# Expert slots handed out in two phases, in a fused attention and mixture-of-experts kernel

## What is computed

```
x = x + conv_ref(ln_c(x))          # keys = queries, softmax over 256 positions, value, output
t = tokens(x);  n = ln_t(t)        # 2048 x 64
probs = softmax(n @ router_w.T);  the top 2 of 8, renormalised, are the gates
h = silu(n @ w1[e].T) * (n @ w3[e].T)      # 682 hidden units per expert
y = h @ w2[e].T
out = t + sum over the two chosen experts of gate * y
```

## Time and profile before

| | us |
|---|---|
| median of 3 runs | 226.94 (225.74 to 230.49) |
| the profiled execution | 226.59 |
| its span in the profile | 224.9 |
| PE busy | 154.0 (69%) |
| DVE busy | 112.0 (50%) |
| POOL busy | 85.5 (38%) |
| ACT busy | 72.3 (32%) |
| DMA moved | 33.47 MB, of it 39 weight loads of 576 KB |

### The profile page before, as it was taken

The page is one execution under the profiler, slowest core; times in us unless marked ns, Lnnn a source line. Parts: engine busy times, 40 slices in busy tenths (PEclk is TensorE's granted clock), DMA queues, the critical chain, the costliest instruction groups (busy, mean ns, idle before and its releaser), DMA issues.

```text
span 224.9 us, 4952 instructions
## 1 busy us (share of the span) xinstructions
PE 154.0 (69%) x1714; PEld 134.1 (60%) x1714; DVE 112.0 (50%) x398; ACT 72.3 (32%) x154; POOL 85.5 (38%) x109
## 2 busy tenths in 40 slices
PE   2647698795835000009999999999999999974040
PEld 2436598694734000007888888888888888862020
DVE  2696687679458640003544555454554545440050
ACT  2226544433001000005444445355444445530010
POOL 6142520204787777710003344333333444352300
PEclk9999755569555555555999999999999999997555
DMA  4999800000000000011067887887878887000153
GB/s 130 431 388 421 342 0 3 0 0 0 26 26 28 30 24 25 29 39 34 3 224 227 265 286 250 292 282 245 270 241 253 265 262 266 24 15 12 38 170 89
DMA packets 16315, 33.47 MB, mean 149 GB/s; under 512 B 7827, under 2 KB 9011, under 8 KB 15779
## 3 DMA queue, kind: packets, MB, share of 16 engines
q1 hardware_dynamic: 14018, 30.80, 40.6%
q0 software_dynamic: 2272, 2.36, 3.2%
HBM read 25.94 MB, written 7.21 MB: 147 GB/s over the span
## 4 chain that ended last, share of the span: by engine, by line
issue 40%; POOL 31%; DVE 11%; PE 9%; DMA 4%; ACT 3%; POOLq 1%; ACTq 0%; SPq 0%
POOL ys L335 16%; POOL xs L294 13%; PE bank L804 2%; DVE xn L478 2%; DMA y_in<-ys 2%; DVE kq_right L510 1%; DVE neg_max L515 1%; PE bank L754 1%; PE bank L770 1%; POOL rstd L278 1%; DMA x_sb<-x_tok 1%; ACT kq_right L355 1%; DMA ys<-y_out,y_row 1%; PE bank L792 1%; DVE t_sb L535 1%
## 5 line engine op out<-in xcount | busy, mean ns | idle before, releaser
L335 POOL DMA_INDIRECT ys<-y_out,y_row x39 | 37.5, 962 | 76.2 <-DVE y_out L722 70.2
L918 PE MATMUL bank<-x_cols,weights 64*128 64x128 f32 x468 | 64.5, 286 | 0.5 <-issue 0.5
L920 PE MATMUL bank<-x_cols,weights 64*128 64x128 f32 x468 | 64.5, 286 | 0.0
L714 DVE TENSOR_TENSOR hid<-bank,act_sb 128x512 f32<-128x512 f32 (+1 forms) x60 | 40.7, 678 | 45.8 <-ACT act_sb L429 36.9
L918 PEld LDWEIGHTS bank<-x_cols,weights 64*128 64x128 f32 x468 | 56.9, 193 | 7.4 <-issue 7.0
L920 PEld LDWEIGHTS bank<-x_cols,weights 64*128 64x128 f32 x468 | 56.9, 193 | 0.0
L429 ACT ACTIVATE act_sb<-bank 128x512 f32<-128x512 f32 (+1 forms) x60 | 35.3, 589 | 43.1 <-PE bank L918 42.3
L294 POOL DMA_INDIRECT xs<-rows,pos x32 | 31.2, 975 | 9.7 <-issue 9.7
L936 PE MATMUL bank<-hid,weights 128*64 128x128 f32 x468 | 30.8, 277 | 3.5 <-ACT y_cols L437 3.5
L936 PEld LDWEIGHTS bank<-hid,weights 128*64 128x64 f32 x468 | 25.8, 137 | 6.1 <-issue 3.8
L898 PE MATMUL bank<-ident,x_pairs 128*128 128x128 f32 x39 | 9.2, 317 | 26.7 <-issue 26.7
(11 more groups left out here) (123 smaller groups left out, 192.5 us busy)
## 6 DMA issues: line engine op xcount, KB each, us to landing
weights<-experts SPq DMA_DIRECT2D x39, 576.0 KB
xs<-zeros SPq DMA_DIRECT2D x4, 1056.0 KB, 8.8
x_in<-xs SPq DMA_DIRECT2D x39, 33.0 KB, 1.7
y_in<-ys SPq DMA_DIRECT2D x4, 256.0 KB, 4.0
ys<-y_out,y_row POOLq DMA_INDIRECT x39
xs<-rows,pos POOLq DMA_INDIRECT x32
out<-result SPq DMA_DIRECT2D x8, 64.0 KB, 2.1
x_sb<-x_tok SPq DMA_DIRECT2D x1, 384.0 KB, 3.6
```

Source lines behind the costliest of these rows:

```text
L335: nc.gpsimd.indirect_dma_start(ys, bass.IndirectOffsetOnAxis(ap=y_row[:, HALVES * i + h:HALVES * i + h + 1], axis=0), y_out[:, i % RING, h ...
L714: nc.vector.tensor_tensor(live(i, hid[:, g % HRING, :]), live(i, H3_BANK[g % 3][:]), live(i, act_sb[:, g % 3, :]), ALU.mult).then_inc(hid_ ...
L918: first_ = nc.tensor.matmul(H1_BANK[g % 2][:, dst], weights[0:C, slot, at:at + P], x_cols[0:C, i % 2, src], start=True, stop=True)
L920: second_ = nc.tensor.matmul(H3_BANK[g % 3][:, dst], weights[C:P, slot, at:at + P], x_cols[C:P, i % 2, src], start=True, stop=True)
```

## The change

The slots are handed out in two phases. Phase 0 opens slots 0 to 7 from the counts of blocks 0 and 1, the first half of the tokens. It gives them to subtiles that are full by then: at least 9 of the kind exist whatever the routing. Phase 1 opens slots 8 to 38 from the final counts, less what phase 0 has used. Both phases have a table, so all 39 slots now have their expert and row from value loads.

On SP, the weight loads of the first eight slots no longer go out at the start. After the first table is ready, SP does for each of pairs 0 to 3 four value loads, the weight loads, for pair 0 a wait for the scatters of blocks 0 and 1 (dispatched[0]), and the x_in loads. Then it waits for the second table, and pairs 4 to 19 follow in the order of before, the first of them with a wait for dispatched[1].

On DVE, the first table (subtiles_of_experts(0), owners_of_slots(0), rows_of_slots(0), 12 instructions) stands between positions(2) and choose(3). The second (used_up and what follows, 26 instructions) is cut in four parts, which stand in the expert stage behind multiply(0) and pair_up(2), multiply(1), multiply(3) and pair_up(3), and multiply(5). The rows of phase 0 are all filled, so that pairs 0 to 3 need no keep. On PE, rank(2) has one more small matmul for the counts, and rank_read and counts_ready are waited for before up(0). ACT preloads the table of silu. The number of slots, the work per slot, the scatters and their order on POOL, and the end are as before.

The diff, cut to its core:

```
--- before.py
+++ after.py
-NX = (K_TOP * CAP - 1) // SUB
-NS = E + NX
+NS = E + (K_TOP * CAP - 1) // SUB
 NT = -(-NS // HALVES)
-MORE = CAP // SUB - 1
+MOST = CAP // SUB
+
+
+KNOWN = (2, NBLK)
+PHASES = len(KNOWN)
+OPENED = (0, 8, NS)
+assert all(OPENED[p + 1] <= -(-(K_TOP * BLK * KNOWN[p] - E * (SUB - 1)) // SUB) for p in range(PHASES - 1))
...
+        def phase_of(k):
+            return next(p for p in range(PHASES) if k < KNOWN[p])
+
+        def pairs_of(p):
+            return range(-(-OPENED[p] // HALVES), -(-OPENED[p + 1] // HALVES))
...
-            for e in range(E):
-                sp.dma_start(weights[:, e, :], experts[e]).then_inc(w_loaded[e], 16)
-
-            sp.wait_ge(dispatched, 16 * TILES * K_TOP)
-            for j in range(E):
-                sp.dma_start(x_in[:, j // HALVES, j % HALVES, :], xs[CAP * j:CAP * j + SUB, :]
-                             ).then_inc(x_in_loaded[j // HALVES], 16)
-            sp.wait_ge(table_ready, 1)
-            for i in range(E // HALVES, NT):
-                owners = [sp.value_load(table[0:1, 0, HALVES * i + h - E:HALVES * i + h - E + 1],
-                                        min_val=0, max_val=E - 1) for h in halves(i)]
-                at = [sp.value_load(table[0:1, 1, HALVES * i + h - E:HALVES * i + h - E + 1],
-                                    min_val=0, max_val=E * CAP - SUB) for h in halves(i)]
-                if i >= XRING:
-                    sp.wait_ge(gated, i - XRING + 1)
-                for h in halves(i):
-                    sp.dma_start(x_in[:, i % XRING, h, :], xs[bass.ds(at[h], SUB), :]).then_inc(x_in_loaded[i % XRING], 16)
-                sp.wait_ge(hid_used, STEPS * (i - WSLOTS // HALVES + 1))
+
+            def load_weights(i, owners):
+                if i >= WSLOTS // HALVES:
+                    sp.wait_ge(hid_used, STEPS * (i - WSLOTS // HALVES + 1))
                 for h in halves(i):
                     s = (HALVES * i + h) % WSLOTS
                     sp.dma_start(weights[:, s, :], experts[bass.ds(owners[h], 1)].rearrange("o p c -> p (o c)")
                                  ).then_inc(w_loaded[s], 16)
+
+            for p in range(PHASES):
+                blocks = KNOWN[p] - (KNOWN[p - 1] if p else 0)
+                sp.wait_ge(table_ready, p + 1)
+                for i in pairs_of(p):
+                    owners = [sp.value_load(table[0:1, 0, HALVES * i + h:HALVES * i + h + 1],
+                                            min_val=0, max_val=E - 1) for h in halves(i)]
+                    at = [sp.value_load(table[0:1, 1, HALVES * i + h:HALVES * i + h + 1],
+                                        min_val=0, max_val=E * CAP - SUB) for h in halves(i)]
+                    if p == 0:
+                        load_weights(i, owners)
+                    if i == pairs_of(p)[0]:
+                        sp.wait_ge(dispatched[p], 16 * TPB * K_TOP * blocks)
+                    if i >= XRING:
+                        sp.wait_ge(gated, i - XRING + 1)
+                    for h in halves(i):
+                        sp.dma_start(x_in[:, i % XRING, h, :], xs[bass.ds(at[h], SUB), :]).then_inc(x_in_loaded[i % XRING], 16)
+                    if p > 0:
+                        load_weights(i, owners)
...
-                            rows[:, TPB * k + t, c, :], None).then_inc(dispatched, 16)
+                            rows[:, TPB * k + t, c, :], None).then_inc(dispatched[phase_of(k)], 16)
...
+            nc.scalar.preload_act_table(ACT.Silu)
...
+                for p in range(PHASES - 1):
+                    if KNOWN[p] == k:
+                        count(p, K_BANK[:, TPB * E:(TPB + 1) * E])
...
+            def count(p, sums):
+                nc.vector.tensor_tensor(taken_by[:, p, :], sums, base[:], ALU.subtract).then_inc(counts_ready, 1)
+
+            def subtiles_of_experts(p):
+                dve.wait_ge(counts_ready, p + 1)
+                last = p == PHASES - 1
+                dims = [P, E, MOST]
+                chain(nc.vector.scalar_tensor_tensor(out=over[:], in0=taken_by[:, p, :].unsqueeze(2).to_broadcast(dims),
+                                                     scalar=float(SUB - 1) if last else 0.0,
+                                                     in1=steps_sub[:].unsqueeze(1).to_broadcast(dims),
+                                                     op0=ALU.add, op1=ALU.is_ge))
+                chain(nc.vector.tensor_reduce(full[:], over[:], AX.X, ALU.add))
+                if p > 0:
+                    chain(nc.vector.tensor_tensor(full[:], full[:], used[:, p - 1, :], ALU.subtract))
+                chain(nc.vector.tensor_tensor(upto_full[:], upto[:], full[:].unsqueeze(1).to_broadcast([P, E, E]),
+                                              ALU.mult))
+                chain(nc.vector.tensor_reduce(ends[:], upto_full[:], AX.X, ALU.add))
+
+            def owners_of_slots(p):
+                own = slice(OPENED[p], OPENED[p + 1])
+                n = OPENED[p + 1] - OPENED[p]
+                chain(nc.vector.tensor_scalar(given[:], ends[:], float(SUB), None, ALU.mult))
+                end = given[:, 0:E - 1].unsqueeze(1).to_broadcast([P, n, E - 1])
+                chain(nc.vector.tensor_tensor(passed[:, own, :], slot_at[:, own].unsqueeze(2).to_broadcast([P, n, E - 1]),
+                                              end, ALU.is_ge))
+                chain(nc.vector.tensor_reduce(owner[:, own], passed[:, own, :], AX.X, ALU.add))
+                nc.vector.tensor_copy(table[:, 0, own], owner[:, own]).then_inc(dve_step, 1)
+                steps[0] += 1
+                chain(nc.vector.tensor_tensor(starts[:, own, :], passed[:, own, :], end, ALU.mult))
+                chain(nc.vector.tensor_reduce(first[:, own], starts[:, own, :], AX.X, ALU.max))
+                chain(nc.vector.tensor_tensor(row_at[:, own], slot_at[:, own], first[:, own], ALU.subtract))
+
+            def rows_of_slots(p):
+                own = slice(OPENED[p], OPENED[p + 1])
+                n = OPENED[p + 1] - OPENED[p]
+                all_e = [P, n, E]
+                if p == 0:
+                    nc.vector.scalar_tensor_tensor(out=table[:, 1, own], in0=owner[:, own], scalar=float(CAP),
+                                                   in1=row_at[:, own], op0=ALU.mult, op1=ALU.add).then_inc(table_ready, 1)
+                    return
+                chain(nc.vector.scalar_tensor_tensor(out=begin[:], in0=used[:, p - 1, :], scalar=float(SUB), in1=base[:],
+                                                     op0=ALU.mult, op1=ALU.add))
+                chain(nc.vector.tensor_tensor(of_owner[:, own, :], order[:].unsqueeze(1).to_broadcast(all_e),
+                                              owner[:, own].unsqueeze(2).to_broadcast(all_e), ALU.is_equal))
+                chain(nc.vector.tensor_tensor(starts_e[:, own, :], of_owner[:, own, :],
+                                              begin[:].unsqueeze(1).to_broadcast(all_e), ALU.mult))
+                chain(nc.vector.tensor_reduce(owned[:, own], starts_e[:, own, :], AX.X, ALU.add))
+                chain(nc.vector.tensor_tensor(owned[:, own], owned[:, own], row_at[:, own], ALU.add))
+                nc.vector.tensor_scalar(table[:, 1, own], owned[:, own], float(E * CAP - SUB), None, ALU.min
+                                        ).then_inc(table_ready, 1)
+
+            def used_up(p):
+                chain(nc.vector.tensor_scalar(given[:], ends[:], float(OPENED[p + 1] - OPENED[p]), None, ALU.min))
+                before_ = slice(0, E - 1)
+                if p == 0:
+                    chain(nc.vector.tensor_copy(used[:, p, :], given[:]))
+                else:
+                    chain(nc.vector.tensor_tensor(used[:, p, :], used[:, p - 1, :], given[:], ALU.add))
+                chain(nc.vector.tensor_tensor(used[:, p, 1:], used[:, p, 1:], given[:, before_], ALU.subtract))
+
+            def occupancy(p):
+                own = slice(OPENED[p], OPENED[p + 1])
+                n = OPENED[p + 1] - OPENED[p]
+                all_e = [P, n, E]
+                chain(nc.vector.scalar_tensor_tensor(out=left[:], in0=used[:, p - 1, :], scalar=-float(SUB),
+                                                     in1=taken_by[:, p, :], op0=ALU.mult, op1=ALU.add))
+                chain(nc.vector.tensor_tensor(of_owner[:, own, :], of_owner[:, own, :],
+                                              left[:].unsqueeze(1).to_broadcast(all_e), ALU.mult))
+                chain(nc.vector.tensor_reduce(owned[:, own], of_owner[:, own, :], AX.X, ALU.add))
+                chain(nc.vector.tensor_tensor(limit[:, own], owned[:, own], row_at[:, own], ALU.subtract))
+                nc.vector.tensor_tensor(keep[:, own], limit[:, own], slot_no[:].to_broadcast([P, n]), ALU.is_gt
                                         ).then_inc(keep_ready, 1)
...
+            subtiles_of_experts(0)
+            owners_of_slots(0)
+            rows_of_slots(0)
             choose(NBLK - 1)
```

(50 more changed lines are left out.)

67 lines of the change are left out of this document (9 added, 58 removed).

## The result

The changed kernel took 233.68 us (median of 233.1, 233.68 and a disturbed 237.68, which the comparison leaves out), the kernel before 226.94. The ratio is 1.037, 95% interval 1.0302 to 1.0438: slower. The profiled execution took 233.1 (span 231.4).

What follows compares the result with a forecast made beforehand. Taken as bound: the last scatter, some 20 pairs at 5.0 us on PE, and a tail. Starting up12 at 114.6 instead of 122.3 saves 7.7 us: 226.6 - 7.7 = 218.9 us, range 211 to 224.

Steps and rivals of the forecast that it cites:

- The SP queue: SP's value loads, weight and x_in issues for pairs 0 to 3: 4.35 us per pair, pair 0's weights at 78.5.
- factor of 1.6: DVE's table chains beside scatters take 1.6 times their sum; the first table so takes 4.6 us.
- up12: PE's first up step of pair 4: starts at 114.6 instead of 122.33, so 7.7 us less.
- for no engine's sake: Tail: ACT's y_cols comes 3.1 us after PE's work ends; in another program up to 3 us less.
- first table ready: DVE, 12 instructions ahead of choose(3): phase 0's table ready at 76.0, bounds 74.3 and 76.5.
- x_in there after weights: DMA queues: a pair's x_in lands 5.0 us after its weights are issued, lower bound 2.17 us after its own issue.
- second table ready: DVE, expert stage: parts end at 103.0, so table and SP release pair 4 7 us later than they could.
- up5: PE's up step that needs m1 and m2: starts at 99.7, then 12.6 us of work and 2.3 for the clock.
- behind up12: PE from pair 4 to the end: all as before, 5.0 us per pair, SP's 4.35 lying below.
- Rival 1: Only the last scatter holds pair 4; tables and value loads find cover: 16.8 us less, 209.8 us; chance 0.15.
- Rival 2: PE's clock rises late, staying at 1.2 GHz through the next pair: 4.5 us more, 223.4 us; chance 0.15.
- Rival 3: DMA queue backs up, SP bounds the whole stage at 5.7 us per pair: 228.7 us, slower; chance 0.05.

Runs made afterwards that it cites:

- e14: Kernel before with 36 unused value loads added on SyncE while the scatters run, on chip 0: 224.04 us.
- e2: Kernel before with 36 unused value loads added on SyncE while the scatters run, on chip 7: 230.15 us (before 227.22).
- e13: Changed kernel, unaltered, run again on chip 0: 216.03 us, ratio 0.9612 to the kernel before.
- e15: Changed kernel with the second table made early on VectorE, scatters not paced, on chip 0: 214.2 us, ratio 0.9537.
- e11: Changed kernel with phase 0's experts and rows as constants, its weights loaded at the start, four scatters in flight, second table early, chip 8: 209.45 us.
- e1: Changed kernel with the scatters of blocks 2 and 3 held until the input of pairs 0 to 3 has landed, chip 7: 235.6 us.
- e4: Changed kernel with at most two scatters of blocks 2 and 3 in flight, chip 7: 225.87 us, 0.994 of before.
- e12: Changed kernel with at most four scatters in flight and the second table early, chip 8: 212.61 us, ratio 0.9515.
- e3: Changed kernel with phase 0's experts and rows as constants and its weights loaded at the start, chip 7: 226.28 us.
- e5: Changed kernel with all 32 scatters paced, two in flight, chip 4: 224.88 us (before 224.53).
- e9: Changed kernel with at most four scatters in flight, second table left late, chip 8: 215.77 us (before 224.33).

## Why the prediction was wrong, and where it was right

**The step that failed** is the one headed "The SP queue": "A pair so costs SP 4.35 us", from the 2.40 us of four value loads that the earlier trace rows show at 113.4 to 115.8, a stretch in which GpSimd issues next to nothing. In the measured execution the four value loads and four issues of a pair ran among back-to-back scatters and took 19.87 us. I had given VectorE's chain beside the scatters a factor of 1.6, and SyncE's beside the same scatters none. The rest follows: the copy of pair 1 came at 107.06 and not at 87.9, up12 at 132.08 and not 114.6, 17.5 us late; behind it the execution needed 231.4 - 132.08 = 99.3 us where I had put 102.6. 17.5 - 3.3 = 14.2, which is 233.1 - 218.9.

**The sign of it could be seen beforehand.** The stall of 0.70 us ahead of L608 has the size of one slow step, and the factor of 1.6 was made of such stalls: the old table, 9.14 us there, takes 75.71 to 81.10 in e14, 5.4 us. y_cols at 204.11, 3.1 us late "for no engine's sake", looks like the same thing: GpSimd had issued four result scatters from 198.24 to 203.1. Both are absent where the chip is quick; e14, the kernel before but for its loads, needs 222.3 - 123.23 = 99.1 us behind its up12, e2 on chip 7 228.4 - 125.93 = 102.5. The first measurement of the changed kernel happened not to have that second stall, and so needed only 99.3. I took the one for the price of work and the other for chance, and asked of neither what it would do to a queue with 24 instructions per pair.

**The same steps where there are no slow steps** (e13 against the forecast):

| step | forecast | e13 |
|---|---|---|
| first table ready | 76.0 | 73.5 |
| weights of pair 0 | 78.5 | 76.16 |
| SyncE per pair | 4.35 | 5.2 |
| x_in there after weights | 5.0 | 7.5 and 8.8 |
| copy of pair 2 | 92.2 | 95.26 |
| second table ready | 103.0 | 103.71 |
| x_in, weights of pair 4 | 105.4, 106.4 | 106.10, 107.14 |
| up5 | 99.7 | 101.13 |
| up12 | 114.6 | 114.63 |
| behind up12 | 102.6 | 99.5 |
| time | 218.9 | 216.0 (profiled 215.8) |

The 2.5 us won at the table (no factor of 1.6: the chain L626 to L656 took 2.8 us) went into slower transfers, as the DMA engines are 0.78 busy from 78 to 84 us and 0.93 from 84 to 98: 7.5 us for pair 0 (76.16 to 83.66) and 8.8 for pair 2 (86.43 to 95.26). up5 was 1.4 late. TensorE's clock, at 0.50 until 103, rose to 0.96 within the next microsecond: from up5 to up12 are 13.5 us, 0.9 and not 2.3 above the 12.6 at full clock. So up12 within 0.1 us of the forecast is luck, made of terms that cancel; the time is 2.9 us better because the stall in the tail is missing, which the forecast had allowed for (-3 to 0). The mechanism is the forecast one: the second table and SyncE's loads release pair 4, and release it in time, since TensorE works almost without a pause from 100.36 to up12. What places up12 is up5, and up5 waits for the copy of pair 2 and for VectorE, which does two parts of the second table ahead of m1 and m2; e15, without them there, has up5 at 98.84. (The forecast's own bounds add up to -9.2 and +2.9 us, 209.7 to 221.8, and not to its 213 to 222; nothing here hangs on that.)

**The rivals.** Rival 1 (209.8) can be reached: e11, whose SyncE doesn't wait for the first table and has the second at 84.6, takes 209.45 in its one execution. That the numbers agree is partly luck: its up12 comes at 108.67, 3.2 us after the 105.5 that the bound implies, and behind it are 99.0 us in place of 102.6. For the change as it is, rival 1 doesn't hold, since pair 4 isn't issued at 98. Rival 2 (the clock) was a small price in both cases: 0.9 us in e13, and in the first measurement from up5 (117.78) to up12 14.3 us, 1.7 above the 12.6. There the clock had risen at 111, was back at 0.50 after 3.4 us without a matmul, and stood there until 121:

```profile
117.00:122.00 5.00, 4.92 (x44) 4.19 (x42) 4.79 (x14) 1.57 (x3) 0.00 (x0) 0.55 0.02 5
```

Rival 3 was my slower case, at 0.05, and it was the wrong mechanism: it wanted full DMA queues and a loss spread over 15 pairs. The loss came from SyncE, but all in pairs 0 and 1; the weights of pairs 2 and 3 followed after 4.5 and 4.7 us, and from 118 on TensorE was the bound as before.

The scatters keep 1.26 us from one to the next in both conditions, beside the table at 72 to 74.7 as beside nothing (91 to 97). Beside this the Trainium skill (SBUF — State Buffer, "SBUF: two separate sides") describes that GpSimd can't write descriptors while VectorE holds the port pair that they share. The runs show nothing of it, with VectorE instructions of 0.2 to 0.7 us (the longest is m0 of e13, at 89.69); longer ones beside the scatters weren't tried.

**What stays open** is what makes a chip slow. Shown: the first measurement and the runs on chip 7 had the slow steps, the four groups on chips 4, 8 and 0 didn't, within a group all kernels agreed, and on chip 7 the steps went where scatters are issued in a row (e1) and ended when the line was kept short (e4). Not shown: whether it is the chip or its state at that hour, since no chip is known to have been seen in both conditions (that of the first measurement isn't recorded); whether the changed kernel itself takes 233 beside a slow probe, since it wasn't run on chip 7; why the steps begin only 17 us after the first scatter in e2; and what the 0.70 us are. Pacing was tried in the slow condition only with two in flight (e4); whether e12's version keeps its gain there wasn't tried, as the last group again fell on a quick chip.

Every time on record comes with a profiled span, so no run shows what the kernel takes without its trace being recorded. The Trainium skill (NOTIFIC — the notification-queue block, "Overflow: three behaviours, one of which stalls the engine") describes that the block which takes the engines' trace records can, in one of its settings, stall the producer while its ring is full. No run here shows it. It would fit steps that reach SyncE, VectorE, ScalarE and in e1 and e3 TensorE; it leaves unsaid why GpSimd keeps its 1.26 us throughout.

## What to carry to other kernels

A stall of fixed size in the trace of before that no work explains (here 0.70 us, or idle time whose releaser is "remote") may belong to a condition, not to the work beside it: ask which queue the change moves under it, and multiply that queue's instructions by it. Where a result contradicts a sum, run the changed kernel again on another chip, with a probe beside it that measures the suspected cost, before explaining.

## What was not expected of the hardware

- A register operation of SyncE, 0.15 to 0.18 us in e13 (L258), took 0.69 to 0.71 us between 84 and 101 us in the slow condition, and one value load there 1.39 us (0.27 in e13).
- The shortest value load gives the condition away: in each of the six slow traces one line of value loads has a minimum of 2 to 15 ns, in the fourteen quick ones none is below 260. The first row is of the kernel before as first measured (L239), the second of e13 (L260):

```profile
L239 SPq TENSOR_LOAD <-table x31: 15/266/414, 103.3 to 184.2; - x31
```

```profile
L260 SPq TENSOR_LOAD <-table x39: 260/267/334, 74.9 to 176.9; - x39
```

- GpSimd's own issue wasn't slowed: 1.26 us from scatter to scatter in both conditions. Pacing does slow it: with two in flight the last scatter begins at 113.77 (e5) instead of 95.51 (e13), with four at 99.69 (e9).
- While scatters and weights are under way together, the DMA engines are busy to 0.93 and move 279 GB/s (e13, 84 to 98 us), and x_in is there 7.5 to 8.8 us after the weights ahead of it are issued.
